# Three edits to a single-core attention and feed-forward kernel: earlier first tiles, path weights and copies by block, and row shifts moved into the turn

## The chip, the core and the metric

The kernel runs on one core of a Trainium2 chip. The engines of the core are TensorE (PE for its matmuls, PEld for its weight loads), VectorE (DVE), ScalarE (ACT), GpSimd (POOL) and SyncE (SP, which here only issues DMAs). Each engine takes its instructions in the order in which the program lists them, and semaphores hold an instruction until another engine or a transfer has counted far enough. The metric is the device time of one execution in microseconds, the median of several.

## What is computed

One block of a perceiver over 64 sequences of 32 rows, width 512: a cross attention with rotated queries, a self attention, and a feed-forward part. The three stretches that matter here are the layer norm of the input, the folding of the feed-forward matrices, and the feed-forward itself.

```python
x = x + xattn(_layernorm(x), ctx_512, Wq, w_kc_q, w_kc_kv, W_qr, W_kr, Wo)
x = x + attn(_layernorm(x), ...)
x = x + ffn(_layernorm(x), ...)

def ffn(x, ...):                      # L = 2 layers, two paths each
    amp = sigmoid(x @ amp_w + amp_b)
    ph = tanh(x @ ph_w + ph_b) * pi
    h = (cos(ph) + sin(ph)) * amp
    for l in range(L):
        e = h @ ent_w[l] + ent_b[l]
        h = layer_norm(h + e @ ent_pw[l] + ent_pb[l], ln3_g[l], ln3_b[l])
        t = einsum('bsd,pdf->pbsf', h, path_w[l]) + path_b[l]
        mod = cos(phase[l]) + sin(phase[l])
        h = layer_norm(h + sum(t * mod, axis=0), ln4_g[l], ln4_b[l])
    return h
```

Since nothing non-linear stands between `ent_w` and `ent_pw`, nor between the two paths and their sum, each layer is two matrices of 512 by 512. The kernel works these four out once ("fold") and the feed-forward then does four products a tile.

## The kernel before

**Query path** (`query_path`). The 2048 input rows are 16 tiles of 128 rows, in four groups of four. DVE measures a group (`measure_group`: mean and variance of each tile, then `invert_group`), ACT takes the root and normalises in place (`normalise_group`), PE transposes (`turn_x`), ACT rounds the transposed tile (`round_x`) and DVE takes the rest of the rounding (`split_x`): all products of this part are three matmuls of a high and a low part. For the first group the order is: DVE measures all four tiles, inverts, does the first `rotate`, then the splits, with `split_wq(0, 0)` between the second and third tile; ACT likewise rounds the first weights between the second and third tile. PE's first product needs all four tiles and the weights. After that come eight head pairs of two units each; within the first unit further groups are turned. ACT's order there is: `store_a(U, 0, 0)`, two key roundings, a weight rounding, `store_a(U, 1, 0)`, and only then `take_groups(i, J, 1)`, which rounds tiles 4 to 7. DVE wants those tiles as the first thing of its step.

**Fold** (`fold_weights`). For each of two layers PE forms `ent_w[l] @ ent_pw[l]` as 16 contraction steps (k) by 4 row blocks (m) of 128 by 512, float32. The first twelve k go over all m in turn; the last four k go block by block, so that block 0 is done first (`block_done`). The weights come from HBM in eight pieces a layer through four buffers; SP's list has the second layer's path matrices (2 MB) ahead of that layer's pieces, and the path load waits for GpSimd to have used the first layer's. Four matrices are finished in the order `STAGES = (0, 1, 3, 2)`: an even one comes from PE, an odd one from GpSimd. ACT copies a block out of PSUM (`copied`), DVE adds the identity, adds to a bias and multiplies by the gain (`finish`, `gained`), ACT rounds it (`rounded`), DVE takes the rest (`split_matrix`). PE's first matmul of layer 1 into block m waits for the copy of block m. Meanwhile DVE has its own sums over the pieces (`sum_entangled`, 16 a layer), on which SP's loads of later pieces wait too. GpSimd multiplies both paths of a layer by their modulation and adds them, in three instructions of 128 by 2048.

**Feed-forward** (`feed_forward`). Four turns of four tiles. A turn is 16 units (step j, tile u): PE's product, DVE's bias and mean (L2118, L2120), ACT's sum of squares and root (L2053, L2055), DVE's normalise (L2125, L2127), PE's transpose for the next step (L1988), ACT's and DVE's rounding (L2047, L77). DVE adds the finished tile of a turn to its row in the first four units of the next (`add_row`, L2133), after GpSimd has multiplied the tile by the gain (L1933) and shifted the row (`shift_rows`, L1925). In turns 0 and 1 GpSimd first normalises tiles two turns ahead, and so its shifts come late in step 1. In turns 2 and 3 there is nothing to normalise, and the four shifts follow the last turn's gains at once.

Of the kernel before, what the change touches and what calls it, by code (L numbers as in the profile page):

```python
# [24 lines left out]
P = 128  # L25
# [54 lines left out]
def query_path(nc, x_s, early, w_qr, w_kr, late, angle_q, centre_q, x1, spare, crossing, ident, eps, w_vo_dram, q_dram):  # L80
# [7 lines left out]
    with ExitStack() as ctx:  # L88
# [203 lines left out]
        def _(dve):  # L292
            def measure_group(g):
                for u in range(4):
                    dve.wait_ge(x_loaded[g % 2][u], 16 * (g // 2 + 1))
                    nc.vector.bn_stats(tallies[:, u], xin[:, g % 2, u]).then_inc(x_tallied, 1)
                for u in range(4):
# [3 lines left out]
            def invert_group(g):  # L301
                dve.wait_ge(x_rooted, g + 1)
                nc.vector.reciprocal(rstd[:], deviation[:]).then_inc(x_inverted, 1)
                dve.wait_ge(x_inverted, g + 1)
                nc.vector.scalar_tensor_tensor(offset[:], moments[:, :, 0], -1.0, rstd[:], ALU.mult, ALU.mult).then_inc(x_offset, 1)
# [82 lines left out]
            measure_group(0)  # L388
            invert_group(0)
            rotate(0, 0, 0)  # L390
            split_x(0)
            split_x(1)
            split_wq(0, 0)
            split_x(2)
            split_x(3)
# [123 lines left out]
        def _(act):  # L519
            def normalise_group(g):  # L520
                act.wait_ge(x_measured, 4 * g + 4)
                nc.scalar.activation(deviation[:], moments[:, :, 1], ACT.Sqrt, bias=eps[:]).then_inc(x_rooted, 1)
                act.wait_ge(x_offset, g + 1)
                for u in range(4):
# [57 lines left out]
            def unit(i, J, final=False):  # L582
# [15 lines left out]
                if J == 1:  # L598
                    take_groups(i, J, 1)
# [9 lines left out]
                if J == 0:  # L609
# [30 lines left out]
            normalise_group(0)  # L640
            round_x(0)
            round_x(1)
            round_wq(0, 0)
            round_x(2)
            round_x(3)
            round_rot(0, 0)
# [965 lines left out]
def fold_weights(nc, loads, path, rows, x2, stat, eps, spare, half_pi, folded, bias, out_norm, ident, gate):  # L1612
# [6 lines left out]
    with ExitStack() as ctx:  # L1619
# [26 lines left out]
        def _(sp):  # L1646
# [7 lines left out]
            for l in range(LAYERS):  # L1654
# [10 lines left out]
                if l == 0:  # L1665
                    sp.wait_ge(pool_chained, PW)
                    sp.wait_ge(summed, 1)
                    sp.dma_start(paths[:], path[1]).then_inc(paths_loaded, 16)
            sp.wait_ge(paths_loaded, 16 * LAYERS)
            sp.wait_ge(summed, LAYERS)  # L1670
# [4 lines left out]
        def _(pool):  # L1675
# [5 lines left out]
            for l in range(LAYERS):  # L1681
                pool.wait_ge(paths_loaded, 16 * (l + 1))
                for p in range(PW):
                    mod = phases[:, l * PW + p].unsqueeze(1).to_broadcast([P, CD, D])
                    nc.gpsimd.tensor_tensor(paths[:, p], paths[:, p], mod, ALU.mult).then_inc(pool_chained, 1)
                pool.wait_ge(pool_chained, PW * (l + 1))
                if l:
                    pool.wait_ge(split, 2 * CD)
# [592 lines left out]
```

## Time and profile before

| | us |
|---|---|
| median of 3 runs | 1568.08 |
| lowest and highest | 1566.51, 1572.47 |
| the profiled execution, whole | 1566.61 |
| its span, first to last instruction | 1564.8 |
| TensorE busy in it | 1459.1 (93%) |
| mean granted TensorE clock | 0.976 |

Times in the trace are microseconds from the start of the span. A timeline row that ends in x4 is four instructions merged, and its duration is that of the four. The bracket at a row's end is the time for which the engine had waited before it, and what released it.

### The profile page before, as it was taken

Reading aid. Unit: us, or ns where it says so; the run is one execution under the profiler, and the core shown is the slowest. Engines: PE = TensorE matmul, PEld = TensorE weight load, DVE = VectorE, ACT = ScalarE, POOL = GpSimd, SP = SyncE. Lnnn points to the kernel's source line nnn. Section 1 sums busy time; section 2 is a strip of 40 time slices with the busy share of each in tenths; the row PEclk is TensorE's granted clock in tenths of the full one; section 3 lists DMA queues with packets and bytes.
Section 4 is the critical chain, followed back from the end, with each engine's and each line's share of the span. In section 5 each row is a group of like instructions: output and inputs, shape, how many; then the busy total and the mean of one; then the engine's idle time right before and its main releaser. Section 6 shows DMA issues by size and latency. Waiting matters only on the chain. (4 is left out here: it accounts for less than half of the span.)

```text
span 1564.8 us, 27392 instructions
## 1 busy us (share of the span) xinstructions
PE 1459.1 (93%) x8399; PEld 1128.9 (72%) x8399; DVE 1136.4 (73%) x1952; ACT 864.4 (55%) x1862; POOL 637.2 (41%) x597
## 2 busy tenths in 40 slices
PE   4799999999977999999999988999889899998997
PEld 3577777777756888888888868888434478787876
DVE  6888788877738888888888855677598634647466
ACT  5566656656556666667666644555211355554544
POOL 4244244524027777777777622220361212312021
PEclk9899999999989999999999999999899899999999
DMA  4224343333386555555656523000354000000000
GB/s 156 68 73 119 107 119 90 103 107 112 101 284 130 112 132 111 132 115 121 131 113 154 111 54 137 0 0 1 121 188 162 1 1 1 28 1 27 0 27 27
DMA packets 140775, 139.84 MB, mean 89 GB/s; under 512 B 84134, under 2 KB 111910, under 8 KB 139564
## 3 DMA queue, kind: packets, MB, share of 16 engines
q1 hardware_dynamic: 140140, 138.30, 32.7%
q10 hardware_dynamic: 576, 0.81, 0.2%
q8 instruction: 30, 0.49, 0.1%
q14 instruction: 29, 0.24, 0.1%
HBM read 109.62 MB, written 27.39 MB: 88 GB/s over the span
## 5 line engine op out<-in xcount | busy, mean ns | idle before, releaser
L1082 ACT ACTIVATE c_sc_ps<-c_sc_ps,c_peak 128x257 f32<-128x257 f32 x256 | 114.1, 446 | 88.4 <-DVE c_peak L966 88.4
L77 DVE TENSOR_TENSOR b_rot_parts_low<-b_rot,b_rot_parts_high 128x1536 fp32r<-128x1536 f32 x64 | 136.4, 2132 | 22.0 <-ACT b_rot_parts_high L545 21.9
L280 POOL TENSOR_TENSOR b_turned_raw<-b_turn_part 128x384 f32<-128x384 f32 x32 | 70.1, 2189 | 164.9 <-DVE b_key_parts_low L77 163.6
L1697 PE MATMUL f_ps<-f_right,f_left 128*128 128x512 f32 x256 | 116.2, 615 | 8.2 <-ACT f_raw L1740 5.9
L929 POOL TENSOR_TENSOR c_mixed_low<-c_whole,c_mixed_high 128x512 fp32r<-128x512 f32 x64 | 81.9, 1279 | 98.1 <-ACT c_mixed_high L1112 98.1
L328 DVE TENSOR_TENSOR b_rot<-b_w_qr,b_angle 128x1536 f32<-128x1536 f32 x64 | 118.3, 1849 | 0.2
L77 DVE TENSOR_TENSOR c_e_t_low<-c_et_ps,c_e_t_high 128x512 fp32r<-128x512 f32 x128 | 87.9, 687 | 39.7 <-ACT c_e_t_high L1090 39.6
L70 PE MATMUL b_ps<-c_shared_high,b_wq_parts_high 128*128 128x512 f32 x256 | 108.4, 424 | 6.5 <-DVE c_shared_low L77 6.5
L276 POOL TENSOR_TENSOR b_turn_part<-b_early,b_centre 128x384 f32<-128x384 f32 x64 | 83.7, 1328 | 71.3 <-DMA b_early<-early 69.6
L70 PE MATMUL e_mm_ps<-folded_high,e_h_t_high 128*128 128x512 f32 x256 | 105.9, 414 | 5.7 <-DVE e_h_t_low L77 5.6
L966 DVE TENSOR_REDUCE c_peak<-c_sc_ps 128x2 f32<-128x514 f32 x128 | 88.5, 691 | 31.3 <-PE c_sc_ps L72 30.8
L545 ACT ACTIVATE b_rot_parts_high<-b_rot 128x1536 fp32r<-128x1536 f32 x64 | 95.2, 1488 | 24.5 <-PE b_ps L72 17.0
L2053 ACT ACTIVATE spare<-spare 128x512 f32<-128x512 f32 x64 | 46.3, 724 | 112.5 <-DVE spare L2120 112.5
L1090 ACT ACTIVATE c_e_t_high<-c_et_ps 128x512 fp32r<-128x512 f32 x128 | 76.5, 598 | 53.9 <-PE c_et_ps L1181 53.9
L70 PE MATMUL c_out_ps<-c_shared_high,c_mixed_high 128*128 128x512 f32 x240 | 104.4, 435 | 0.0
L1697 PEld LDWEIGHTS f_ps<-f_right,f_left 128*128 128x128 f32 x256 | 50.0, 197 | 74.2 <-issue 65.1
L72 PE MATMUL b_ps<-c_shared_high,b_wq_parts_low 128*128 128x512 f32 x256 | 103.5, 404 | 0.0
L71 PE MATMUL b_ps<-c_shared_low,b_wq_parts_high 128*128 128x512 f32 x256 | 103.0, 403 | 0.0
L1933 POOL TENSOR_TENSOR spare<-spare,out_norm 128x512 f32<-128x512 f32 x15 | 20.9, 1392 | 199.4 <-DVE spare L2127 199.4
L71 PE MATMUL e_mm_ps<-folded_low,e_h_t_high 128*128 128x512 f32 x256 | 101.9, 398 | 0.0
L72 PE MATMUL e_mm_ps<-folded_high,e_h_t_low 128*128 128x512 f32 x256 | 101.8, 398 | 0.0
L1181 PE MATMUL c_et_ps<-ident,c_e 128*128 128x128 f32 x512 | 80.1, 279 | 20.1 <-DVE c_e_t_low L77 15.7
(270 smaller groups left out, 4330.9 us busy)
## 6 DMA issues: line engine op xcount, KB each, us to landing
c_ends_spread<-end_weights SPq DMA_DIRECT2D x63, 256.0 KB, 3.8
carried_queries<-x SPq DMA_DIRECT2D x7, 2048.0 KB, 11.3
b_early<-early SPq DMA_DIRECT2D x15, 640.0 KB, 4.0
c_raw<-cache_t SPq DMA_DIRECT2D x64, 128.5 KB, 3.5
c_swapped<-cache_t SPq DMA_DIRECT2D x128, 64.2 KB, 3.2
f_left<-ent_in SPq DMA_DIRECT2D x16, 512.0 KB, 5.4
f_right<-ent_out SPq DMA_DIRECT2D x16, 512.0 KB, 6.5
c_q_first<-carried_queries SPq DMA_DIRECT2D x32, 224.0 KB, 3.4
```

Of the source, the lines that this page charges most:

```text
L70: nc.tensor.matmul(out, left[0], right[0], start=start, stop=False)
L71: nc.tensor.matmul(out, left[0], right[1], start=False, stop=False)
L72: return nc.tensor.matmul(out, left[1], right[0], start=False, stop=stop)
L77: return nc.vector.tensor_tensor(low, value, high.bitcast(F32), ALU.subtract)
L276: nc.gpsimd.tensor_tensor(turn_part[:, n], key, centre[:, 2 * v + n].unsqueeze(2).to_broadcast(shape), ALU.mult).then_inc(key_multiplied, 1)
L328: nc.vector.tensor_tensor(rot[:, k % 2], weight, angles, ALU.mult).then_inc(rot_ready, 1)
L545: nc.scalar.activation(rot_parts[0][:, k % 2], rot[:, k % 2], ACT.Copy).then_inc(rot_rounded, 1)
L929: nc.gpsimd.tensor_tensor(mixed[1][:, w, :, u], whole[:, u % 2].rearrange("p (h s) -> p h s", h=H), mixed[0][:, w, :, u].bitcast(F32), ALU ...
L966: nc.vector.tensor_reduce(peak[:, v], sc_ps[:, 2 * v:2 * v + 2, 0:L], AX_X, ALU.max, negate=True).then_inc(peaked, 1)
L1082: last = nc.scalar.activation(sc_ps[:, 2 * v + c, 0:L], sc_ps[:, 2 * v + c, 0:L], ACT.Exp, bias=peak[:, v, c:c + 1], accum_out=total[:, v, ...
L1181: last = nc.tensor.transpose(et_ps[:, (2 * k + c) * P:(2 * k + c + 1) * P], e[:, half, c, k * P:(k + 1) * P], ident[:])
L1697: return nc.tensor.matmul(ps[:, m], left[:, slot, m * P:(m + 1) * P], right[:, slot], start=k == 0, stop=k == CF - 1)
```

## The change

It has three places.

*First group.* DVE measures and inverts tiles 0 to 2, does the first `rotate`, and then measures and inverts tile 3; ACT normalises three tiles, rounds tile 0, normalises tile 3 and rounds the other three, with the weight rounding behind all four. DVE splits all four before the weights. In the first unit `take_groups(0, 0, 1)` moves ahead of the key roundings.

*Fold.* In stage 0 ACT copies block m + 1 out before it rounds block m. GpSimd takes the paths by row blocks of 128 by 512 (two products and one addition each, twelve instructions a layer for three), `summed` counts blocks, and DVE waits for its block only. SP waits for all four.

*Feed-forward.* In the last two turns a row shift waits for the normalise of tile u in step 1.

```diff
-            measure_group(0)
-            invert_group(0)
+            measure_group(0, range(3))
+            invert_group(0, slice(0, 3))
             rotate(0, 0, 0)
-            split_x(0)
-            split_x(1)
+            measure_group(0, range(3, 4))
+            invert_group(0, slice(3, 4))
+            for t in range(4):
+                split_x(t)
             split_wq(0, 0)
-            split_x(2)
-            split_x(3)
...
-                if J == 1:
+                if J == 1 or begins:
                     take_groups(i, J, 1)
...
-                if J == 0:
+                if J == 0 and not begins:
                     take_groups(i, J, 1)
...
-            normalise_group(0)
+            normalise_group(0, slice(0, 3))
             round_x(0)
+            normalise_group(0, slice(3, 4))
             round_x(1)
-            round_wq(0, 0)
             round_x(2)
             round_x(3)
+            round_wq(0, 0)
...
                 if l == 0:
-                    sp.wait_ge(pool_chained, PW)
-                    sp.wait_ge(summed, 1)
+                    sp.wait_ge(summed, CD)
                     sp.dma_start(paths[:], path[1]).then_inc(paths_loaded, 16)
...
-                for p in range(PW):
-                    mod = phases[:, l * PW + p].unsqueeze(1).to_broadcast([P, CD, D])
-                    nc.gpsimd.tensor_tensor(paths[:, p], paths[:, p], mod, ALU.mult).then_inc(pool_chained, 1)
-                pool.wait_ge(pool_chained, PW * (l + 1))
-                if l:
-                    pool.wait_ge(split, 2 * CD)
-                nc.gpsimd.tensor_tensor(raw[:, 1], paths[:, 0], paths[:, 1], ALU.add).then_inc(summed, 1)
+                for c in range(CD):
+                    for p in range(PW):
+                        nc.gpsimd.tensor_tensor(paths[:, p, c], paths[:, p, c], phases[:, l * PW + p], ALU.mult).then_inc(pool_chained, 1)
+                    pool.wait_ge(pool_chained, PW * (CD * l + c + 1))
+                    if l and c == 0:
+                        pool.wait_ge(split, 2 * CD)
+                    nc.gpsimd.tensor_tensor(raw[:, 1, c], paths[:, 0, c], paths[:, 1, c], ALU.add).then_inc(summed, 1)
...
+            def round_block(n, j, m):
+                act.wait_ge(gained, CD * n + m + 1)
+                nc.scalar.activation(folded[0][:, j, m], raw[:, j % 2, m], ACT.Copy).then_inc(rounded, 1)
...
-                    if j % 2 == 0:
-                        act.wait_ge(block_done, CD * (j // 2) + m + 1)
+                    if j == 0:
+                        act.wait_ge(block_done, m + 1)
                         nc.scalar.activation(raw[:, 0, m], ps[:, m], ACT.Copy).then_inc(copied, 1)
-                    act.wait_ge(gained, CD * n + m + 1)
-                    nc.scalar.activation(folded[0][:, j, m], raw[:, j % 2, m], ACT.Copy).then_inc(rounded, 1)
+                        if m:
+                            round_block(n, j, m - 1)
...
-                    elif m == 0:
-                        dve.wait_ge(summed, j // 2 + 1)
+                    else:
+                        dve.wait_ge(summed, CD * (j // 2) + m + 1)
...
                     pool.wait_ge(fetched, t + 1)
+                    if isinstance(i, int) and i + 2 >= TURNS:
+                        pool.wait_ge(y_normed, UNITS * i + G + u + 1)
                     nc.gpsimd.tensor_tensor(row_of(t), row_of(t), out_norm[:, 1], ALU.add).then_inc(shifted, 1)
```

ACT in the first unit of the query path, before. L550 copies a product (`p_sb`), L555 a projection (`q_sb`), L535 rounds keys, L545 rotated weights, L530 the transposed input tiles.

```order
20 L550 ACTIVATE spare<-b_ps 128x512 [waits b_multiplied]
21 L555 ACTIVATE x<-b_ps 128x512 [waits b_projected]
22 L535 ACTIVATE b_key_parts_high<-b_turned_raw 128x384 [waits b_key_ready] x2
23 L545 ACTIVATE b_rot_parts_high<-b_rot 128x1536 [waits b_multiplied,b_rot_ready]
24 L555 ACTIVATE x<-b_ps 128x512 [waits b_projected]
25 L530 ACTIVATE c_shared_high<-b_ps 128x4x128 [waits b_x_turned] x4
```

The same place now:

```order
22 L553 ACTIVATE spare<-b_ps 128x512 [waits b_multiplied]
23 L558 ACTIVATE x<-b_ps 128x512 [waits b_projected]
24 L533 ACTIVATE c_shared_high<-b_ps 128x4x128 [waits b_x_turned] x4
25 L538 ACTIVATE b_key_parts_high<-b_turned_raw 128x384 [waits b_key_ready] x2
26 L548 ACTIVATE b_rot_parts_high<-b_rot 128x1536 [waits b_multiplied,b_rot_ready]
27 L558 ACTIVATE x<-b_ps 128x512 [waits b_projected]
```

The four tile roundings moved ahead of four instructions.

ACT in the fold's first stage, before (L1740 is the copy out of PSUM, L1742 the rounding):

```order
559 L1740 ACTIVATE f_raw<-f_ps 128x512 [waits b_qr_stored,b_vo_done]
560 L1742 ACTIVATE folded_high<-f_raw 128x512 [waits b_m_stored]
561 L1740 ACTIVATE f_raw<-f_ps 128x512 [waits b_qr_stored]
562 L1742 ACTIVATE folded_high<-f_raw 128x512 [waits b_m_stored]
563 L1740 ACTIVATE f_raw<-f_ps 128x512 [waits b_qr_stored]
```

The same place now (L1747 the copy, L1741 the rounding; the semaphores carry recycled names):

```order
561 L1747 ACTIVATE f_raw<-f_ps 128x512 [waits b_qr_stored,b_vo_done]
562 L1747 ACTIVATE f_raw<-f_ps 128x512 [waits b_qr_stored]
563 L1741 ACTIVATE folded_high<-f_raw 128x512 [waits b_m_stored]
564 L1747 ACTIVATE f_raw<-f_ps 128x512 [waits b_qr_stored]
565 L1741 ACTIVATE folded_high<-f_raw 128x512 [waits b_m_stored]
```

Each copy after the first now stands one rounding earlier.

## Rows read from the trace of the kernel before

**Rows 1.** the page's first part: busy time, share of the span, instructions

```profile
PE 1459.1 (93%) x8399; PEld 1128.9 (72%) x8399; DVE 1136.4 (73%) x1952; ACT 864.4 (55%) x1862; POOL 637.2 (41%) x597
```

**Rows 2.** waits of PE, us 0 to 110: total us, times, longest

```profile
PE b_ps L70 <- DVE c_shared_low L77: 6.5, 2, 3.9
```

**Rows 3.** timeline of DVE, start: us, us of duration, instruction, wait

```profile
9.60 0.69 DVE L296 BATCH_NORM_STATS2 b_tallies<-x 128x6 f32<-128x512 f32 x1 [1.85 <-DMA x<-x_s]
...
11.60 1.74 DVE L328 TENSOR_TENSOR b_rot<-b_w_qr,b_angle 128x1536 f32<-128x1536 f32 x1
...
18.64 1.97 DVE L77 TENSOR_TENSOR b_rot_parts_low<-b_rot,b_rot_parts_high 128x1536 fp32r<-128x1536 f32 x1
...
36.05 2.48 DVE L77 TENSOR_TENSOR c_shared_low<-b_ps,c_shared_high 128x512 fp32r<-128x512 f32 x4 [3.79 <-ACT c_shared_high L530]
```

**Rows 4.** timeline of ACT, the same stretch

```profile
11.71 2.93 ACT L526 ACTIVATE x<-x,b_offset,b_rstd 128x512 f32<-128x512 f32 x4 [0.80 <-DVE b_offset L305]
...
32.75 0.93 ACT L535 ACTIVATE b_key_parts_high<-b_turned_raw 128x384 fp32r<-128x384 f32 x2
...
35.43 2.05 ACT L530 ACTIVATE c_shared_high<-b_ps 128x512 fp32r<-128x512 f32 x4
```

**Rows 5.** waits of all engines, us 1100 to 1240

```profile
PE f_ps L1697 <- ACT f_raw L1740: 5.9, 3, 4.7
```

**Rows 6.** fold: us, busy of five engines (instructions), PEclk, DMA share, GB/s

```profile
1163.40:1200.80 37.40, 31.51 (x65) 12.90 (x65) 31.16 (x42) 6.50 (x11) 9.36 (x2) 0.86 0.40 140
1202.50:1230.00 27.50, 27.50 (x66) 12.19 (x65) 18.21 (x33) 6.20 (x10) 0.00 (x0) 1.00 0.27 111
```

**Rows 7.** timelines of POOL and DVE in the fold

```profile
1136.12 9.88 POOL L1685 TENSOR_TENSOR paths<-paths,f_phases 128x2048 f32<-128x2048 f32 x2 [17.29 <-issue]
...
1136.02 15.44 DVE L1807 TENSOR_TENSOR spare<-spare,f_phases 1x512 f32<-1x512 f32 x4
1151.49 6.26 DVE L1761 SCALAR_TENSOR_TENSOR spare<-f_right,f_col,spare 128x512 f32<-128x512 f32 x8
```

**Rows 8.** all row shifts of GpSimd: ns, min/median/max

```profile
L1925 POOL TENSOR_TENSOR x<-x,out_norm x16: 1258/1383/1747, 1297.0 to 1513.4; 128x512 f32<-128x512 f32 x16
```

**Rows 9.** timeline of SP in the fold; in the last row us to landing

```profile
1150.98 0.33 SPq L1668 DMA_DIRECT2D paths<-path  x1
...
1153.48 0.44 SPq L1603 DMA_DIRECT2D f_right<-ent_out  x1
...
f_right<-ent_out SPq DMA_DIRECT2D x1, 512.0 KB, 7.5
```

**Rows 10.** waits of PE at the starts of turns 2 and 3

```profile
PE e_turn_ps L1988 <- DVE spare L2127: 5.3, 2, 4.0
PE e_mm_ps L70 <- DVE e_h_t_low L77: 1.7, 3, 1.1
```

**Rows 11.** timelines of POOL and DVE, feed-forward; L2118 over all turns (ns)

```profile
1428.66 5.86 POOL L1925 TENSOR_TENSOR x<-x,out_norm 128x512 f32<-128x512 f32 x4
...
1430.36 1.82 DVE L2133 TENSOR_TENSOR x<-x,spare 128x512 f32 x1
...
1433.27 1.53 DVE L2127 TENSOR_SCALAR spare<-spare 128x512 f32<-128x512 f32 x1
1434.72 0.68 DVE L2133 TENSOR_TENSOR x<-x,spare 128x512 f32 x1
...
1440.68 0.55 DVE L2127 TENSOR_SCALAR spare<-spare 128x512 f32<-128x512 f32 x1
...
L2118 DVE SCALAR_TENSOR_TENSOR spare<-e_mm_ps,bias x64: 681/692/693, 1274.4 to 1556.9; 128x512 f32<-128x512 f32 x64
```

**Rows 12.** behind PE waits of 2.54, 1.99, 3.96 us; columns as rows 6

```profile
53.60:55.60 2.00, 1.96 (x9) 1.99 (x10) 0.70 (x2) 0.60 (x1) 0.00 (x0) 0.50 0.00 0
...
72.90:74.50 1.60, 1.53 (x10) 1.29 (x11) 0.76 (x2) 0.87 (x2) 0.00 (x0) 1.00 0.00 0
...
1434.00:1438.00 4.00, 3.07 (x10) 2.64 (x11) 2.87 (x7) 1.85 (x6) 0.52 (x1) 0.57 0.00 0
```

More of the change, by code:

```diff
@@ L292, in _, with measure_group, invert_group @@
         def _(dve):
-            def measure_group(g):
-                for u in range(4):
+            def measure_group(g, us=range(4)):
+                for u in us:
                     dve.wait_ge(x_loaded[g % 2][u], 16 * (g // 2 + 1))
                     nc.vector.bn_stats(tallies[:, u], xin[:, g % 2, u]).then_inc(x_tallied, 1)
-                for u in range(4):
+                for u in us:
                     dve.wait_ge(x_tallied, 4 * g + u + 1)
                     nc.vector.bn_aggr(moments[:, u], tallies[:, u]).then_inc(x_measured, 1)
[L301 to L305, printed above, removed]
+            def invert_group(g, us=slice(0, 4)):
+                step = g + (us.stop == 4)
+                dve.wait_ge(x_rooted, step + 1)
+                nc.vector.reciprocal(rstd[:, us], deviation[:, us]).then_inc(x_inverted, 1)
+                dve.wait_ge(x_inverted, step + 1)
+                nc.vector.scalar_tensor_tensor(offset[:, us], moments[:, us, 0], -1.0, rstd[:, us], ALU.mult, ALU.mult).then_inc(x_offset, 1)
             def split_x(t):
@@ L519, in _, with normalise_group @@
         def _(act):
[L520 to L524, printed above, removed]
+            def normalise_group(g, us=slice(0, 4)):
+                act.wait_ge(x_measured, 4 * g + us.stop)
+                nc.scalar.activation(deviation[:, us], moments[:, us, 1], ACT.Sqrt, bias=eps[:]).then_inc(x_rooted, 1)
+                act.wait_ge(x_offset, g + (us.stop == 4) + 1)
+                for u in range(us.start, us.stop):
                     tile = xin[:, g % 2, u]
@@ L1665, in _ @@
                 if l == 0:
-                    sp.wait_ge(pool_chained, PW)
-                    sp.wait_ge(summed, 1)
+                    sp.wait_ge(summed, CD)
                     sp.dma_start(paths[:], path[1]).then_inc(paths_loaded, 16)
             sp.wait_ge(paths_loaded, 16 * LAYERS)
-            sp.wait_ge(summed, LAYERS)
+            sp.wait_ge(summed, CD * LAYERS)
             gate.load(sp)
@@ L1734, in _ @@
             act.wait_ge(cosined, 2)
+            def round_block(n, j, m):
+                act.wait_ge(gained, CD * n + m + 1)
+                nc.scalar.activation(folded[0][:, j, m], raw[:, j % 2, m], ACT.Copy).then_inc(rounded, 1)
             for n, j in enumerate(STAGES):
                 for m in range(CD):
-                    if j % 2 == 0:
-                        act.wait_ge(block_done, CD * (j // 2) + m + 1)
+                    if j == 0:
+                        act.wait_ge(block_done, m + 1)
                         nc.scalar.activation(raw[:, 0, m], ps[:, m], ACT.Copy).then_inc(copied, 1)
-                    act.wait_ge(gained, CD * n + m + 1)
-                    nc.scalar.activation(folded[0][:, j, m], raw[:, j % 2, m], ACT.Copy).then_inc(rounded, 1)
+                        if m:
+                            round_block(n, j, m - 1)
+                    elif j == 2:
+                        act.wait_ge(block_done, CD + m + 1)
+                        nc.scalar.activation(raw[:, 0, m], ps[:, m], ACT.Copy).then_inc(copied, 1)
+                        round_block(n, j, m)
+                    else:
+                        round_block(n, j, m)
+                if j == 0:
+                    round_block(n, j, CD - 1)
         @block.vector
@@ L1773, in finish @@
                         dve.wait_ge(copied, CD * (j // 2) + m + 1)
-                    elif m == 0:
-                        dve.wait_ge(summed, j // 2 + 1)
+                    else:
+                        dve.wait_ge(summed, CD * (j // 2) + m + 1)
                     square = matrix[:, m, m * P:(m + 1) * P]
```

## The prediction

> **What bounds the kernel now.** I read the page's first part, then the waits of TensorE, then timelines around the three places that the change touches. TensorE is busy 1459.1 us, 93% of the span [rows 1], so outside a few stretches the kernel is as long as its matmuls, and an edit pays only where PE stands still or runs at its lower clock. There are three such places, and each is set by the DVE chain or by something that holds it up.
>
> At the start PE waits twice for split input tiles, 6.5 us in all, 3.9 in the longer wait [rows 2]. In the fold PE waits 5.9 us for copies out of PSUM [rows 5], the first half of layer 1 takes 37.4 us, and the second half, with as many matmuls, 27.5 [rows 6]. The 9.9 us between them are the 5.9 of waiting and 4.0 at the lower clock (granted 0.86 over the first half, 1.00 over the second). At the starts of turns 2 and 3 PE waits 5.3 us for a normalise and 1.7 for a split, 4.0 of it in one piece [rows 10].
>
> **First group.** DVE has three tiles measured at 7.75 and then waits 1.85 for tile 3, which comes at 9.60; the first rotate follows at 11.60 and takes 1.74 [rows 3]. From the end of the measuring (9.60 + 0.69) to the rotate are 1.3 us of aggregates, root and inverse. Now the three are inverted by 7.75 + 1.3 = 9.05, the rotate ends near 10.8, tile 3 is measured by 11.5 and inverted by 12.8; ACT has by then normalised three (4 in 2.93, so 2.2) and rounded one [rows 4]. I take 13.0. Before, the inverse was ready at 11.6 and the chain to `split_rot` (18.64 [rows 3]) took 7.0. It now holds three normalises (2.2) and one rounding (0.5) less: 13.0 + 4.3 = 17.3. That is 1.3 us sooner, and DVE is busy from there until it measures group 1. The weight rounding put last costs nothing beyond this; it is in the 4.3. Bounds: 0, if DVE's inverse of tile 3 stands behind a GpSimd instruction, and 2.2.
>
> `take_groups` moved forward: the four instructions that stood ahead of the tile roundings ran from 32.75 to 35.43 [rows 4], and DVE waited 3.79 for the first rounded tile, until 36.05 [rows 3]. The transposes are long done. The roundings move up 35.43 - 32.75 = 2.7 us and DVE with them. The key and weight roundings now come 2.05 later, under DVE's 2.48 of tile splits, so they are hidden; were they not, half a microsecond would be lost. DVE then works without a gap through the next group, whose normalised tiles PE waits for, so the 2.7 stays. Start: 1.3 + 2.7 = **4.0 us**, bounds 1.5 and 5.
>
> **Fold.** Two instructions of GpSimd over 2048 elements took 9.88, and the addition 4.83 more to 1150.9; beside them four tiny DVE products (1 x 512) took 15.44 us, one per GpSimd instruction, and only then came the eight sums (6.26) [rows 7]. In blocks of 512 a DVE instruction waits for a fourth as long. The nearest rows for the new instruction are the sixteen row shifts, same shape: 1258 ns at least, 1747 at most [rows 8]. Four of them in a row, with three two-input DVE instructions between, took 5.86 [rows 11], which is 0.27 us per change of hands; the slowest shift says 0.49. So GpSimd's stream of twelve takes 12 x 1.26 + 12 x (0.27 to 0.49) + 0.4 for its waits on itself = 18.7 to 21.4, and ends at 1154.8 to 1157.5; I take 1155.8, near the lower, which has several instructions behind it. DVE gets one instruction in per GpSimd instruction: twelve (four products, eight sums) in the same 19.7 us, done near 1155, where before they were done at 1157.75.
>
> The copies: PE's layer 0 ends at 1163.4, its blocks 3.45 us apart (four of sixteen k, 27.5 / 8). With the copy ahead of the rounding, the copy of block 2 (due 1160.0) waits only for gain 0 (DVE near 1157), and the copy of block 3 for gain 1. All 5.9 us of waiting for copies go, and with them the lower clock: 9.9 us.
>
> What is late next is the data. SP has the second path load ahead of layer 1's pieces, and it now waits for the twelfth GpSimd instruction: 1155.8, not 1150.98. Before, the first piece was there at 1153.48 + 7.5 = 1161.0, that is 10.0 behind the path's issue [rows 9]; now at 1165.8. PE is ready at 1163.4 and waits 2.4 us. Fold: 9.9 - 2.4 = **7.5 us**. Whether 2.4 us of waiting lets the clock fall is open: behind a wait of 1.99 it stood at 1.00, behind one of 2.54 at 0.50 [rows 12]. I take no fall; with one it is 1.3 to 4.0 less. Bounds 3.5 and 9.9. The later pieces hang on DVE's sums, which start some 8 us sooner and have slack; GpSimd's second layer leaves ten instructions beside them, and only `finish(3, 2)`, 20 us on, wants their result.
>
> **Feed-forward.** Beside the four shifts (5.86 from 1428.66) DVE's row addition took 1.82 where its neighbour took 0.68, and its normalise 1.53 where it takes 0.55 [rows 11]: 1.1 + 1.0 = 2.1 us on the chain for which PE waits 4.0. The wait shrinks to 1.9, short enough to keep the clock, which then stood at 0.57 over 4 us [rows 12]: 1.3 more. Turn 3 has the same pair of collisions and waits of 5.3 + 1.7 - 4.0 = 3.0 [rows 10]; I take 2.1 again. The shifts themselves now begin right behind a normalise in step 1, run 1.26, and the next instruction of DVE that could collide is the next normalise, 3.2 us or more later; between lie reads of PSUM like L2118, whose 64 take 681 to 693 ns whatever GpSimd does [rows 11]. Cost 0; without that cover 8 x up to 1.0. Feed-forward: 2.1 + 1.3 + 2.1 = **5.5 us**, bounds 3 and 7.5.
>
> The Trainium skill (SBUF — State Buffer, "Who interferes with whom") says that a VectorE instruction with two SBUF inputs contends with GpSimd's reads and that the later one blocks for the whole instruction. On DVE's side the trace agrees (four tiny products in 15.44 us); on GpSimd's side it shows 0.27 to 0.49 us a change, not a whole DVE instruction.
>
> **Sum.** 4.0 + 7.5 + 5.5 = 17.0 us off the profiled execution of 1566.6: 1549.6. The median of the runs is 1.5 above that execution, so the forecast is **1551**.
>
> **Rivals.** (a) A change of hands costs a whole DVE instruction (0.78, a sum alone [rows 7]): twelve GpSimd instructions take 12 x 2.04 + 0.4 = 24.9, the path goes out at 1161, PE waits 7.6 and its clock falls, the fold gains nothing to 2; total gain about 10.5, 1557.5. For it: DVE's side of rows 7. Against it: 5.86 for four would have been 6.9. This is the skill's rule named above. (b) The start gives nothing, since tile 3's inverse and rounding come as late as before, or later gaps swallow it: gain 13, 1555. Against it: DVE has no gap between its first splits and group 1. (c) The shifts in step 1 collide after all: 8 x 0.7 = 5.6 lost, 1556.5. Against it: the next two-input instruction is far. (d) No data wait at all, if GpSimd ends by 1153.4: gain 19.4, 1548.5; it would take 1.4 us a pair. (e) Slower: SP's list behind the path load. Should a block instruction cost GpSimd a fixed time that the shifts don't show, each microsecond on the stream is one on PE: from 3.1 us apiece (1136.1 + 37) the lost wait eats all 17; at 3.4 it ends at 1177, PE waits 24, and the time is 1572. Against it: sixteen rows of the same shape, none above 1.75. (f) The edits don't do what they say, because the copies still wait for gains: then DVE's sums end as before and the gain is 9.5 or so, 1558.5.
>
> **How the numbers follow.** Forecast (1547 to 1554 by its own bounds) 0.55; (a) 0.11; (b) 0.09; (c) 0.07; (d) 0.08; (e) 0.04; (f) 0.06. A measurement of this kernel tells 0.5%, 7.8 us, from no change, so faster is below 1560.2. Faster: all but (e) and a third of (a) and (f): 0.90; same 0.07; slower 0.03. The lowest bounds together (1.5 + 3.5 + 3 = 8) give 1560, the highest (5 + 9.9 + 7.5 = 22.4) 1545.7. The range 1545.5 to 1560 leaves out (e), part of (a) and (f).
>
> **What the profile after would show.** Right: DVE's fifth to eighth splits start near 32 and PE waits under 2 us before the projection that follows; the four 1 x 512 products take some 5 us, not 15.44; no wait of L1697 for ACT, but one of 2 to 3 us for a piece near 1159 (4.0 sooner than 1163.4, plus its wait); the first half of layer 1 within 30 us; L2127 at 0.55 and L2133 at 0.68 at the starts of turns 2 and 3. Wrong: a path load issued more than 21 us after GpSimd's first block, a lower clock behind it, or L2127 over 0.6 in step 1 of turns 2 and 3.

## The result and the profile after

| | before | after |
|---|---|---|
| median, us | 1567.78 (6 runs) | 1554.88 (6 runs) |
| lowest and highest | 1566.51, 1572.47 | 1552.40, 1558.49 |
| profiled execution, whole | 1566.61 | 1555.35 |
| its span | 1564.8 | 1553.5 |
| ratio over all runs | | 0.9912, 95% interval 0.9900 to 0.9924 |

The changed kernel is 12.9 us faster by the medians, 13.8 by the ratio and 11.3 by the two profiled executions. The forecast was 1551.0 with a range of 1545.5 to 1560.0 and 17.0 us of gain: side and range held, and the gain is about three quarters of what was forecast.

The page's first part, beside [rows 1]. TensorE's busy time has hardly moved; what went is time in which it stood.

```profile
PE 1457.0 (94%) x8399; PEld 1128.5 (73%) x8399; DVE 1129.7 (73%) x1954; ACT 864.6 (56%) x1863; POOL 643.9 (41%) x615
```

**The start.** Waits of PE from 0 to 76 us (total, times, longest), then timelines of DVE and ACT (start, duration, instruction, in brackets the wait before it), beside [rows 2 to 4]:

```profile
PE b_ps L70 <- DVE b_rot_parts_low L77: 3.2, 2, 2.6
...
PE b_ps L70 <- DVE c_shared_low L77: 1.2, 1, 1.2
```

```profile
8.86 1.75 DVE L330 TENSOR_TENSOR b_rot<-b_w_qr,b_angle 128x1536 f32<-128x1536 f32 x1
...
12.10 0.16 DVE L307 SCALAR_TENSOR_TENSOR b_offset<-b_moments,b_rstd 128x1 f32<-128x1 f32 x1
...
16.83 2.03 DVE L77 TENSOR_TENSOR b_rot_parts_low<-b_rot,b_rot_parts_high 128x1536 fp32r<-128x1536 f32 x1 [0.27 <-ACT b_rot_parts_high L548]
...
24.08 2.46 DVE L296 BATCH_NORM_STATS2 b_tallies<-x 128x6 f32<-128x512 f32 x4
...
32.25 2.48 DVE L77 TENSOR_TENSOR c_shared_low<-b_ps,c_shared_high 128x512 fp32r<-128x512 f32 x4 [1.10 <-ACT c_shared_high L533]
```

```profile
31.64 2.04 ACT L533 ACTIVATE c_shared_high<-b_ps 128x512 fp32r<-128x512 f32 x4
```

Tile 3 is inverted at 12.1, `split_rot` begins at 16.83 (18.64 before), and the splits of group 1 begin at 32.25 (36.05 before), because the roundings do (31.64 against 35.43). PE's wait of 3.9 for them is 1.2 now.

**The fold.** Timelines of PE, SP, POOL and DVE, and a window over the first half of layer 1 (us, busy of PE, PEld, DVE, ACT and POOL with instructions, granted clock, DMA share, GB/s), beside [rows 5 to 7, 9]:

```profile
1104.02 56.62 PE L1700 MATMUL f_ps<-f_right,f_left 128*128 128x512 f32 x128 [2.35 <-PEq L1270]
1163.94 29.43 PE L1700 MATMUL f_ps<-f_right,f_left 128*128 128x512 f32 x64 [3.30 <-DMA f_right<-ent_out]
...
1194.93 27.63 PE L1700 MATMUL f_ps<-f_right,f_left 128*128 128x512 f32 x64
```

```profile
1153.77 0.33 SPq L1671 DMA_DIRECT2D paths<-path  x1
...
1154.62 0.43 SPq L1607 DMA_DIRECT2D f_right<-ent_out  x1
```

```profile
1133.62 3.38 POOL L1688 TENSOR_TENSOR paths<-paths,f_phases 128x512 f32<-128x512 f32 x2 [17.29 <-issue]
1137.07 1.60 POOL L1692 TENSOR_TENSOR f_raw<-paths 128x512 f32<-128x512 f32 x1
...
1152.15 1.59 POOL L1692 TENSOR_TENSOR f_raw<-paths 128x512 f32<-128x512 f32 x1
```

```profile
1133.52 5.70 DVE L1822 TENSOR_TENSOR spare<-spare,f_phases 1x512 f32<-1x512 f32 x4
1139.26 13.36 DVE L1776 SCALAR_TENSOR_TENSOR spare<-f_right,f_col,spare 128x512 f32<-128x512 f32 x8
```

```profile
1163.94:1193.37 29.43, 29.43 (x65) 13.02 (x66) 28.53 (x32) 3.15 (x5) 16.93 (x11) 0.94 0.56 202
```

No copy holds PE up. It waits 3.30 us for the first piece of layer 1, and the 64 matmul instructions behind it (two to a product here) take 29.43, where the 64 of the second half take 27.63. The granted clock was 0.88 up to 1178 and 1.00 from there on. Against kernel 4 below, where nothing waits, the loss comes to 1.9 us. GpSimd's stream of twelve ends at 1153.74, 20.1 us after its first block.

**The feed-forward.** Timelines of POOL and DVE in turn 2 and PE's waits at the starts of turns 2 and 3, beside [rows 10, 11]:

```profile
1439.81 1.29 POOL L1942 TENSOR_TENSOR x<-x,out_norm 128x512 f32<-128x512 f32 x1 [17.93 <-DVE spare L2144]
```

```profile
1420.67 1.76 DVE L2150 TENSOR_TENSOR x<-x,spare 128x512 f32 x1 [0.15 <-issue]
...
1423.54 0.69 DVE L2150 TENSOR_TENSOR x<-x,spare 128x512 f32 x1
```

```profile
PE e_turn_ps L2005 <- DVE spare L2144: 2.2, 2, 1.8
PE e_mm_ps L70 <- DVE e_h_t_low L77: 1.2, 3, 0.5
```

The shifts now run in step 1 and the row addition takes 0.69. The first addition of a turn still takes 1.76, since it meets GpSimd's last gain.

### The profile page after: what moved, and what is told of

Same layout as the page of the kernel before. It is cut to its first block and busy times, and to the rows that moved or that the text cites. A ratio compares the mean times of both kernels' runs of the same rounds, so it can differ in the third digit from the quotient of the medians.

```text
span 1553.5 us, 27420 instructions
## 1 busy us (share of the span) xinstructions
PE 1457.0 (94%) x8399; PEld 1128.5 (73%) x8399; DVE 1129.7 (73%) x1954; ACT 864.6 (56%) x1863; POOL 643.9 (41%) x615
## 5 line engine op out<-in xcount | busy, mean ns | idle before, releaser
L72 PE MATMUL c_out_ps<-c_shared_high,c_mixed_low 128*128 128x512 f32 x240 | 94.5, 394 | 0.0
## 6 DMA issues: line engine op xcount, KB each, us to landing
carried_queries<-x SPq DMA_DIRECT2D x7, 2048.0 KB, 11.3
```

Of the source, the lines that this page charges most:

```text
L72: return nc.tensor.matmul(out, left[1], right[0], start=False, stop=stop)
```

## The experiments

Seven kernels hold a part of the change, put into the kernel before; two hold the change and one or two edits more, and were run twice; one is the changed kernel again. Ratios are to the kernel before on the same chip, and a gain in us behind a ratio is worked out from it. In the first four, theory A is the reading of the two traces above.

**1. The start alone.** Both edits of `query_path`, nothing else.

```diff
-            measure_group(0)
-            invert_group(0)
+            measure_group(0, range(3))
+            invert_group(0, slice(0, 3))
             rotate(0, 0, 0)
+            measure_group(0, range(3, 4))
+            invert_group(0, slice(3, 4))
...
-                if J == 1:
+                if J == 1 or begins:
                     take_groups(i, J, 1)
```

> Only the edits to the start are made to the kernel before (first group of tiles measured in three and one, the four roundings ahead of the weight rounding, take_groups moved behind). Theory A (the start gains 3.8 us up to the wait at 69 us, and TensorE's lower clock behind that wait takes 1.3 of it back, every time): the product that waits for the first split rotation starts near 62.7 (66.5 before), the wait of about 2.0 us before the transposes near 69 is followed by a granted clock of about 0.57 over 4 us, and the whole gain is 2.4 us, 1565.4. Theory B (the lower clock behind that wait is an accident of one run): the same start, a clock of 1.00 behind the wait, gain 3.8 us, 1564.0. Prediction on record for this part: 4.0.

Measured: 1565.80 us, ratio 0.9973 (0.9962 to 0.9984), which is 4.2 us (2.5 to 6.0; 3.3 by the medians). Windows of the start-alone kernel and of the changed kernel, and PE's transposes behind the wait of 2 us in each:

```profile
62.00:67.00 5.00, 4.17 (x19) 3.03 (x21) 5.00 (x5) 1.54 (x2) 0.00 (x0) 0.66 0.00 0
```

```profile
70.83 1.23 PE L415 MATMUL b_ps<-ident,x 128*128 128x128 f32 x8 [1.98 <-DVE c_shared_low L77]
```

```profile
69.00:73.00 4.00, 3.86 (x14) 3.44 (x15) 2.67 (x5) 2.62 (x4) 0.00 (x0) 0.57 0.01 4
```

```profile
69.14 1.80 PE L415 MATMUL b_ps<-ident,x 128*128 128x128 f32 x8 [1.99 <-DVE c_shared_low L77]
```

With the start alone the clock stood at 0.66 between 62 and 67 us and at 1.00 behind the wait; in the changed kernel it was full until that wait and 0.57 behind it. Theory A is out: the lower clock behind the wait near 70 does not come every time, and its gain of 2.4 us lies just outside the interval. Theory B's 3.8 lies inside. A stretch at the lower clock is there in both kernels, in another place, and neither theory had that.

**2. The fold alone.** All of the fold's edits, nothing else.

> Only the edits to the fold are made to the kernel before (copies ahead of the roundings, GpSimd's path products in blocks of 512). Theory A: the 5.9 us of waits for copies and 4.0 of lower clock go; TensorE then waits about 3.3 us for the first piece of layer 1 and loses about 1.9 at the lower clock behind it: the fold gains 5.1 us, the entry to the feed-forward gives 0.7 back, time near 1563. Theory B (the fold's own gain is larger and what comes before it shifts the pieces): wait under 2.5 us and clock 1.00 behind it, gain 7.5, 1560.3. If a hand-over cost GpSimd a whole VectorE instruction: its twelve instructions take over 24 us instead of 20.1, wait over 7 us, gain under 2.

Measured: 1562.86, ratio 0.9959 (0.9943 to 0.9974), 6.4 us (4.1 to 8.9, which holds both theories); the fold itself took 124.5 us against 129.1. PE in the first half of layer 1:

```profile
1167.24 29.43 PE L1696 MATMUL f_ps<-f_right,f_left 128*128 128x512 f32 x64 [2.16 <-DMA f_right<-ent_out]
```

The wait is shorter here (2.16), since layer 0 lost more at the lower clock (58.24 us for 128 instructions, 56.62 in the changed kernel), but the 64 behind it again take 29.43. The wait alone would fit theory B; the clock behind it and the fold's 4.6 us are theory A's. GpSimd's stream is 20.1 us again: a hand-over does not cost it a whole DVE instruction.

**3. The shifts alone.**

```diff
                     pool.wait_ge(fetched, t + 1)
+                    if isinstance(i, int) and i + 2 >= TURNS:
+                        pool.wait_ge(y_normed, UNITS * i + G + u + 1)
```

> Only the edit to the feed-forward is made to the kernel before: the row shifts of the last two turns that have them wait for the normalises of step 1. Theory A: TensorE's wait at the start of turn 2 falls from 4.0 to about 1.8 us, that at the start of turn 3 by about as much, the lower clock before lay mostly under TensorE's own waiting and gives only 0.2: gain 4.4 us, 1563.4. Theory B (prediction on record for this part: 1.3 us more from the clock in turn 2): gain 5.5, 1562.3. Rival C (the shifts collide in step 1): VectorE's normalises of 0.55 us there take over 0.8 us and the gain is under 2.

Measured: 1565.07, ratio 0.9969 (0.9958 to 0.9980), 4.9 us; the feed-forward took 325.1 us against 329.2. PE's waits for the normalise over the whole feed-forward, 5.9 with a longest of 4.0 before:

```profile
PE e_turn_ps L1990 <- DVE spare L2129: 2.7, 3, 1.8
```

Rival C is out. Between A (4.4) and B (5.5) the interval does not choose (3.1 to 6.6 us); the stages further down, with 4.6 us in the feed-forward, are nearer to A.

**4. The pieces ahead of the path.** The changed kernel with two pieces of layer 1 issued before the second path load.

```diff
                         loads.piece(sp, l, q)
-                if l == 0:
-                    sp.wait_ge(summed, CD)
-                    sp.dma_start(paths[:], path[1]).then_inc(paths_loaded, 16)
+                    if l == 1 and q == 1:
+                        sp.wait_ge(summed, CD)
+                        sp.dma_start(paths[:], path[1]).then_inc(paths_loaded, 16)
```

> The changed kernel with one more edit: SyncE issues pieces 0 and 1 of layer 1 ahead of the second path load. Theory A (TensorE's wait of 3.3 us at 1163.9 and the 1.9 us at the lower clock behind it are the price of SyncE's order alone): piece 0 is issued near 1143, no wait for data, clock 1.00 throughout, first half of layer 1 in 27.6 us, gain over the changed kernel 5.2 us, about 1549.7. Theory B (another thing is nearly as late: VectorE's sums that free the slots, or the path load of 2 MB beside the pieces): TensorE still waits 1.5 us or more before or within the first half of layer 1, gain under 3, 1552 or more. Theory C (the path arrives later and TensorE's last bias products wait for GpSimd's second sums): the wait moves behind 1190.

Measured: 1550.29, ratio 0.9876 (0.9857 to 0.9895). SP, PE and a window over the first half of layer 1:

```profile
1142.98 0.43 SPq L1607 DMA_DIRECT2D f_right<-ent_out  x1
...
1153.72 0.33 SPq L1671 DMA_DIRECT2D paths<-path  x1
```

```profile
1103.98 84.19 PE L1700 MATMUL f_ps<-f_right,f_left 128*128 128x512 f32 x192 [2.35 <-PEq L1270]
```

```profile
1160.00:1188.00 28.00, 28.00 (x66) 12.35 (x65) 25.93 (x31) 4.26 (x7) 15.84 (x10) 1.00 0.55 190
```

The 192 matmul instructions of layer 0 and of half of layer 1 are one row without a wait. The granted clock was 0.74 over their first 6 us, as in the changed kernel (0.75), and 1.00 from 1110 on. The fold takes 118.9 us, 5.2 less than in the changed kernel: 3.3 of wait and 1.9 of clock, as theory A had it. Both were the price of one line of SP's list.

**5. The copies alone.** ACT's new order, with GpSimd's three long instructions as before.

```diff
                 for m in range(CD):
-                    if j % 2 == 0:
-                        act.wait_ge(block_done, CD * (j // 2) + m + 1)
+                    if j == 0:
+                        act.wait_ge(block_done, m + 1)
                         nc.scalar.activation(raw[:, 0, m], ps[:, m], ACT.Copy).then_inc(copied, 1)
+                        if m:
+                            round_block(n, j, m - 1)
...
```

> Only the order of copies and roundings is changed in the kernel before; GpSimd keeps its three instructions of 2048 elements. Theory A (the copies waited for VectorE's gains, which GpSimd's long instructions hold up, and one copy more ahead helps little): gain 0 still ends near 1163.5 behind a GpSimd instruction of the second path, copy 2 follows at 1164 and copy 3 waits for gain 1 until about 1170; TensorE still waits about 5 us for a copy, the fold gains 0 to 3 us, time 1566 to 1569. Theory B (the order of the copies alone was the fault, as the prediction's step reads): all copies are out by 1164, the path is issued at 1151 as before, so no data wait either, and the fold gains 9.9: 1559.

Measured: 1568.06, ratio 0.9986 (0.9973 to 0.9999); the fold took 126.1 us, about 3 less. DVE, ACT and PE:

```profile
1158.82 4.61 DVE L1789 TENSOR_TENSOR f_raw<-f_raw,ident 128x128 f32<-128x128 f32 x1
1163.46 4.88 DVE L1790 SCALAR_TENSOR_TENSOR spare<-f_raw,f_col,spare 128x512 f32<-128x512 f32 x1
```

```profile
1169.43 0.58 ACT L1744 ACTIVATE f_raw<-f_ps 128x512 f32<-128x512 f32 x1
```

```profile
1170.06 27.38 PE L1697 MATMUL f_ps<-f_right,f_left 128*128 128x512 f32 x58 [4.58 <-ACT f_raw L1744]
```

An addition over 128 x 128, 0.29 alone, takes 4.61 beside GpSimd's first long instruction of the second layer's paths, and the next DVE instruction 4.88 beside the second. Gain 1 comes at 1168.9, and only then is copy 3 reached. Theory A: the order of the copies alone was not the fault. (A had gain 0 late as well; it was out at 1158.9, and gain 1 alone was held up.)

**6. The blocks alone.** GpSimd's blocks of 512, with ACT's old order.

```diff
-                for p in range(PW):
-                    mod = phases[:, l * PW + p].unsqueeze(1).to_broadcast([P, CD, D])
-                    nc.gpsimd.tensor_tensor(paths[:, p], paths[:, p], mod, ALU.mult).then_inc(pool_chained, 1)
+                for c in range(CD):
+                    for p in range(PW):
+                        nc.gpsimd.tensor_tensor(paths[:, p, c], paths[:, p, c], phases[:, l * PW + p], ALU.mult).then_inc(pool_chained, 1)
...
```

> Only GpSimd's blocks of 512 (and the waits that go with them) are put into the kernel before; ScalarE keeps its old order, each copy behind the rounding of the block before. Theory A (the blocks do it all): VectorE's sums end near 1155, gain m comes 2.1 us behind copy m, less than the 3.45 us between blocks, so no copy is late: TensorE waits for no copy, but 2 to 3.3 us for piece 0, fold gain 4.6 to 5.1 as with both edits, about 1563. Theory B (both edits are needed): TensorE waits 1 us or more for ScalarE at the start of layer 1 on top, fold gain under 4.

Measured: 1563.28, ratio 0.9952 (0.9935 to 0.9969); fold 123.9 us. PE in the first half of layer 1:

```profile
1170.88 29.43 PE L1696 MATMUL f_ps<-f_right,f_left 128*128 128x512 f32 x64 [3.19 <-DMA f_right<-ent_out]
```

The same row as in the changed kernel, without the new order of the copies. The blocks are the whole of the fold's gain as measured (123.9 us, 124.1 to 124.5 with both edits).

The copies still came later here, which theory A had not expected. The last of them:

```profile
1168.43 0.58 ACT L1739 ACTIVATE f_raw<-f_ps 128x512 f32<-128x512 f32 x1
```

It begins 0.7 us behind the end of layer 0 (1167.69); in the changed kernel it begins right behind it (1160.68 and 1160.64). That would cost nothing without the wait for the piece either: a product is two instructions of 0.43 us in the trace, so TensorE would want block 3 only 2.6 us behind the end of layer 0, near 1170.3, and the copy ends at 1169.01. By this estimate the new order adds nothing to the blocks; no run has the blocks and the early pieces with the old order.

**7 and 8. One row addition earlier; the changed kernel again.** Kernel 4 with the first row addition of a turn issued ahead of the last normalise of the turn before.

```diff
-                    if q < G and later(i):
+                    if 0 < q < G and later(i):
                         add_row(i - 1, q)
...
                     split_gated(i + 1, G - 1)
+                    add_row(i, 0)
                 normalise(i, UNITS - 1)
```

> The changed kernel with pieces 0 and 1 ahead of the path load, and one more edit: the first row addition of the next turn is issued ahead of the last normalise of a turn, so that GpSimd's gain does not meet it. Theory A (the 1.84 us that TensorE still waits at the start of turn 2 hold 1.1 us of the row addition of 1.76 us against 0.68 alone): that row addition takes 0.68 to 0.8, the wait falls to 0.8 us, the waits for L2144 sum to 1.0 instead of 2.7, and the kernel is 1 to 2 us faster than with the pieces alone, about 1548.7. Theory B (something else on VectorE meets the gain, or the wait for GpSimd moves into the chain): the wait stays over 1.5, no gain.

> The changed kernel itself once more, as the measure beside the others: ratio 0.991 to the kernel before. Theory A on the clock (in the first 76 us it falls in every execution for some 10 to 13 us in all, but at places that differ): the transposes that wait 1.99 us near 70 start between 69 and 71 us, and the step from there to 1104 us makes up the difference. Theory B: they start at 69.1 with the lower clock behind them, as in its first profile.

Measured: 1549.08, ratio 0.9858 (0.9839 to 0.9878), and for the changed kernel again 1554.73, ratio 0.9902 (0.9882 to 0.9921). DVE and PE at the start of turn 2 of kernel 7, and PE's waits for the normalise over the feed-forward:

```profile
1416.73 0.68 DVE L2150 TENSOR_TENSOR x<-x,spare 128x512 f32 x1
...
1419.13 0.85 DVE L2150 TENSOR_TENSOR x<-x,spare 128x512 f32 x1
```

```profile
1421.76 0.65 PE L2005 MATMUL e_turn_ps<-ident,spare 128*128 128x128 f32 x4 [0.65 <-DVE spare L2144]
```

```profile
PE e_turn_ps L2005 <- DVE spare L2144: 1.9, 3, 0.6
```

The addition takes 0.68 instead of 1.76 and the wait of 1.84 is 0.65: theory A on the mechanism. The three waits for the normalise sum to 1.9 us, not to A's 1.0 (2.7 in kernel 4). On the clock the changed kernel's second profile had its transposes at 68.57, just ahead of A's 69 to 71, and with 1.23 us for eight of them at full clock; theory B is out. Over the first 76 us the granted clock was 0.91 there, 0.89 in its first profile and 0.93 in the kernel before.

**9 and 10. The two edits of the start apart.** The first group's edit alone, and `take_groups` alone.

> Only the first group's edit is made to the kernel before (three tiles inverted first, the fourth behind them, weight rounding last); take_groups stays where it was. Theory A (the prediction's split of the start: 1.3 us here): the first projection of TensorE starts near 16.6 (18.9 before), VectorE measures group 1 about 1.1 us sooner, its splits of group 1 still wait for the roundings behind take_groups, and the gain at the transposes near 70 is 1.1 us, about 1568 against 1569.5. Theory B (the group's part is lost in VectorE's wait for those roundings): gain 0.

> Only take_groups is moved behind the roundings; the first group is measured as before. Theory A (the prediction's 2.7 us): VectorE's splits of group 1 start 2.7 us sooner, near 33.4, TensorE's wait of 3.9 us falls to about 1.2, the transposes near 70 come 2.7 us sooner, about 1566.8 against 1569.5. Theory B (it gives more alone, up to the 3.8 that both give together, because it covers the group's part): 3.8.

Measured: 1568.09, ratio 0.9999 (0.9987 to 1.0011), and 1565.64, ratio 0.9985 (0.9975 to 0.9994). DVE's splits of group 1, first in kernel 9, then in kernel 10, 36.05 in [rows 3]:

```profile
34.93 2.48 DVE L77 TENSOR_TENSOR c_shared_low<-b_ps,c_shared_high 128x512 fp32r<-128x512 f32 x4 [3.78 <-ACT c_shared_high L533]
```

```profile
33.25 2.48 DVE L77 TENSOR_TENSOR c_shared_low<-b_ps,c_shared_high 128x512 fp32r<-128x512 f32 x4 [1.11 <-ACT c_shared_high L530]
```

1.1 us sooner by the one, 2.8 by the other, and 3.8 by both: at this row they add, as A has it in either, and the transposes near 70 keep it (72.97 before, 71.83, 70.16, 69.14 with both). In the whole time kernel 10 shows 2.4 us; what kernel 9 brings cannot be told from nothing there, nor in stage A of the table below (463.4 and 463.3).

**11 and 12. Kernels 4 and 7 once more, on one chip.**

> The changed kernel with pieces 0 and 1 ahead of the path load, beside the next kernel on the same chip: ratio to the kernel before 0.9876 as measured once, fold of 118.9 us from its first product to the transposes of the feed-forward (124.1 in the changed kernel), feed-forward of 325.1 us.

> The same with the first row addition of a turn ahead of the last normalise. Theory A: fold 118.9 us, feed-forward 323.8 us (1.3 us less than without the row edit, one third of it at each of three turn starts or most at turn 2), ratio 0.9865. Theory B (the 1.3 us of the first profile were scatter between executions): feed-forward over 324.8.

Measured: 1549.90, ratio 0.9881 (0.9863 to 0.9900), and 1548.34, ratio 0.9884 (0.9865 to 0.9903). The ratios don't tell them apart; the stages do (325.2 and 323.7 us in the feed-forward, 325.1 and 323.8 the first time).

**The stages of all profiled executions**, in us: A from the span's start to GpSimd's first row `c_kv_t<-spare` (its key addition, near 460), B from there to the fold's first product, C to the first transpose of the feed-forward, D to the end.

| kernel | A | B | C | D |
|---|---|---|---|---|
| before | 463.3 | 643.3 | 129.1 | 329.2 |
| 9 group | 463.4 | 647.9 | 128.8 | 330.4 |
| 10 take | 461.3 | 644.3 | 129.1 | 329.0 |
| 1 start | 460.8 | 643.6 | 128.9 | 330.5 |
| 5 copies | 463.2 | 642.8 | 126.1 | 330.5 |
| 6 blocks | 464.1 | 647.0 | 123.9 | 330.1 |
| 2 fold | 463.0 | 643.9 | 124.5 | 329.4 |
| 3 shifts | 465.3 | 644.7 | 128.9 | 325.1 |
| after | 460.8 | 643.2 | 124.1 | 325.4 |
| 8 after again | 458.6 | 644.0 | 124.3 | 325.6 |
| 4, 11 pieces | 460.1, 460.7 | 643.9, 642.5 | 118.9, 119.0 | 325.1, 325.2 |
| 7, 12 pieces and row | 459.3, 460.6 | 647.5, 643.2 | 119.0, 119.0 | 323.8, 323.7 |

B is the same code in all fourteen and lies between 642.5 and 647.9; A varies by 2.3 with the same code. C varies by 0.6 at most and D by 1.5. So a part of a few microseconds is read from its own stage over several executions, not from two spans. The means: A 463.8 without the start's edits (5 executions) and 460.1 with both (7), 3.7 less; C 129.0 without the fold's edits (5) and 124.2 with blocks (4), 4.8 less; D 329.9 (7) and 325.3 (5), 4.6 less. Together 13.1, beside 12.9 by the medians and 13.8 by the ratio.

## Why the prediction was right, and where its sum was too large

The three parts came out at 3.7, 4.8 and 4.6 us for 4.0, 7.5 and 5.5. All three were forecast too large, so no error made up for another; the range was wide enough for their sum.

**Start: 4.0 forecast, 3.7 measured.** The first group: tile 3 was inverted at 12.1 where the prediction took 13.0, and `split_rot` began at 16.83 where it took 17.3, 1.8 sooner than before. Of that 0.6 went to a key split of 1.18 us at 18.78 that took 0.55 before, so that 1.1 was left at group 1 (24.08 against 25.19, and the same 24.08 in kernel 9). `take_groups`: 2.7 forecast, 2.8 in kernel 10. Rival (b), that the start gives nothing, is out by kernel 1 (2.5 to 6.0 us).

**Fold: 7.5 forecast, 4.8 measured.** Its 9.9 of waits and clock did go (kernel 4 has 118.9 us for the 129.0 of the kernels without these edits), and 3.3 + 1.9 came in their place; the prediction had put in 2.4 for the wait and nothing for the clock (1.3 to 4.0 should it fall, which holds the 1.9). The step that failed is "I take no fall": it rested on [rows 12], where the clock stood at 1.00 behind a wait of 1.99 and at 0.50 behind one of 2.54. In all four kernels that wait for the piece (2.16 to 3.30) the next 64 instructions take 29.43. The wait was mis-sized by 0.9: GpSimd's stream took 20.1 and not 19.7, PE's layer 0 ended 0.3 sooner against it, and piece 0 landed 10.2 behind the path's issue and not 10.0. The size of the hand-over was right: 1.67 us from one GpSimd instruction to the next against 1.26 alone (two in 2.53 in kernel 6), 0.41, between the 0.27 and 0.49 of the prediction. It took the stream near the lower bound, and that bound was an average over three meetings of which one cost GpSimd nothing: of the four shifts from 1428.66 on the two that met a row addition took 1.73 and 1.72, the others 1.28 and 1.26. The third DVE instruction, the normalise at 1433.27, has one tensor as input and not two, as the prediction counted. So rival (a) and the rule behind it are out: the rule of the Trainium skill (SBUF — State Buffer, "Who interferes with whom"), that the later one blocks for the whole instruction, holds on DVE's side (eight sums in 13.36, one per GpSimd instruction, 0.78 apiece alone) and not on GpSimd's, where it would have made the twelve 24.9 us.

One reason was wrong though the number was not, and that part was luck: the prediction said that the copies were freed by being put ahead of the roundings. In kernel 6 they hold nothing up without that, because with DVE not held up they follow one another every 2.8 us (1162.86, 1165.65, 1168.43) and the blocks are 3.45 apart; kernel 5 shows that without GpSimd's blocks the new order gives about 3. Rival (f) said that the copies still wait for gains; that is what kernel 5 does, and not what the change does.

**Feed-forward: 5.5 forecast, 4.6 measured.** The two terms for the start of turn 2 were exact. PE there, before and after:

```profile
1434.93 1.11 PE L1988 MATMUL e_turn_ps<-ident,spare 128*128 128x128 f32 x4 [3.96 <-DVE spare L2127]
1439.49 0.60 PE L1948 MATMUL e_input_ps<-ident,e_xn 128*128 128x128 f32 x4
...
1457.86 0.60 PE L1988 MATMUL e_turn_ps<-ident,spare 128*128 128x128 f32 x4
```

```profile
1426.01 0.65 PE L2005 MATMUL e_turn_ps<-ident,spare 128*128 128x128 f32 x4 [1.84 <-DVE spare L2144]
1429.30 0.60 PE L1965 MATMUL e_input_ps<-ident,e_xn 128*128 128x128 f32 x4
...
1434.49 0.50 PE L70 MATMUL e_mm_ps<-folded_high,e_h_t_high 128*128 128x512 f32 x1 [0.49 <-DVE e_h_t_low L77]
...
1445.83 0.50 PE L70 MATMUL e_mm_ps<-folded_high,e_h_t_high 128*128 128x512 f32 x1 [0.28 <-DVE e_h_t_low L77]
...
1448.73 0.60 PE L2005 MATMUL e_turn_ps<-ident,spare 128*128 128x128 f32 x4
```

PE stopped at 1430.97 before and at 1424.17 after. To the first input transpose it took 8.52 then and 5.13 now: 3.4 us, the 2.1 + 1.3 of the prediction. But the last rows lie 9.13 apart and the second ones 10.19: 1.1 us is given back within five units, through waits for the splits and units of 3.78 us instead of 3.67. The missing step is the one that the prediction takes in the fold and leaves out here: with the stall gone, what is late next? By the two waits shown it is the split of the turned tile; that PE now comes to these products sooner than ACT and DVE hand them their tiles is the reading of these rows, and no run tests it. Turn 3 gave its 2.1: GpSimd's first gain behind it starts at 1540.83 instead of 1552.05, 11.2 sooner, and the one ahead of it 9.1 sooner (1490.46 and 1499.59). The cost of the shifts in step 1 was 0, as forecast: the normalises there take 0.55, and rival (c) is out by kernel 3. These terms sum to 4.4 (2.1 + 1.3 - 1.1 + 2.1). The pair of profiles shows 3.7 in D, since its first tiles give another 0.75 back: the changed kernel is 7.56 us ahead at the first transpose of the feed-forward and 6.81 at the same transpose 47 us on (1283.01 and 1276.20). Such differences come and go with the clock, as shown below. The whole pair shows 11.3 and not 13.1 because A differs by only 2.4 in it and D by 3.7, where the means differ by 3.7 and 4.6.

Rivals (d) and (e) did not come: the wait for data is there (against (d)), and no block of GpSimd took above 1.72 (against (e)).

## What to carry to other kernels

When a wait is removed, follow every engine on to the next late thing, also within the next few units, and give a new wait of 2 to 3 us on TensorE a price for its clock: here 1.9 us behind the wait for the piece every time, and often nothing behind other waits of about 2 us. Look at the issue list of a queue before the compute: here two piece loads stood behind a 2 MB load whose first sum GpSimd could not form until 21 us after its issue (1174.84, behind a split of DVE), and moving them gave 5.2 us, more than any of the three edits. And a long GpSimd instruction costs most by the VectorE instructions that each wait for one: cutting it into blocks was worth 5 us though GpSimd itself took 5 us longer.

## What the runs showed of the hardware that was not expected

- **The lower clock does not go by the length of a wait alone.** Behind the wait of 1.98 to 1.99 us near 70 the transposes ran at full clock in eleven executions (1.22 or 1.23 us for eight) and at the lower one in three (1.80, 1.90 and 1.68; granted 0.57). Behind a wait of 1.84 in turn 2 it did not fall in any of five profiles (0.65 us for four transposes); behind the waits of 2.16 to 3.30 for the piece it fell in all four. Behind one and the same wait of 2.07 or 2.08 at the head of the feed-forward eight transposes took anything from 1.06 us (kernel 2) to 1.94 (the changed kernel). The Trainium skill (TensorE: Matmul & The Clock Gate, "Part 1: The HAM clock gate") says that the number of slow matmuls differs from run to run of one kernel; these runs agree. One row at full clock is no ground for a sum.
- **A small DVE instruction can wait out a whole GpSimd instruction**: 128 x 128 took 4.61 instead of 0.29 in kernel 5, and a `tensor_scalar` with one tensor as input took 1.53 instead of 0.55 [rows 11]. The 64 instructions of L2135, which read PSUM and a bias, took 681 to 694 ns in the changed kernel, whatever GpSimd did.
- **The early transfers did not slow the products**: with the same 2 MB path load and 1 MB pieces in another order the products from 1110 to 1188 in kernel 4 ran at a clock of 1.00 without a gap, beside 189 and 190 GB/s.
